# One decoder layer on one core: latents split from PSUM by two engines, row normalisation as one activation

## The reference, cut to what matters

```python
def _layernorm(x, axis=-1, eps=1e-05):
    m = jnp.mean(x, axis=axis, keepdims=True)
    v = jnp.var(x, axis=axis, keepdims=True)
    return (x - m) / jnp.sqrt(v + eps)

x = x + attn(_layernorm(x), wq, wk, wv, wo)          # causal, 32 query heads, 8 key heads, head size 16
x = x + xattn(_layernorm(x), ctx, Wq_d, W_qk, Wkv_d, Wv_u)
x = x + ffn(_layernorm(x), gate, kernel, bias, lora_A, lora_B, lora_A_shared, lora_B_shared)

def xattn(Q, K, Wq_d, W_qk, Wkv_d, Wv_u):
    C_kv = K @ Wkv_d                                 # the latents: 1500 x 32 for each sequence
    CqWqk = ((Q @ Wq_d) @ W_qk).reshape(b, n, 16, 32)
    scores = einsum('bnhl,bkl->bhnk', CqWqk, C_kv) / sqrt(32)
    V_up = (C_kv @ Wv_u).reshape(b, nkv, 16, 32)
    return einsum('bhnk,bkhd->bnhd', softmax(scores), V_up)
```

## Time and profile before

| | |
|---|---|
| median of three executions | 643.73 us (642.36 to 645.56) |
| the profiled execution | 645.84 us, span 644.0 us |
| mean granted TensorE clock | 0.968 |
| TensorE busy | 584.1 us, 91% |
| VectorE busy | 432.5 us, 67% |
| GpSimd busy | 412.7 us, 64% |
| ScalarE busy | 302.1 us, 47% |

### The profile page before, as it was taken

One profiled execution on the slowest core, in us unless ns is written; L12 is line 12 of the kernel. 1 busy time (PEld: TensorE's weight loads), 2 busy tenths in 40 slices (PEclk: granted clock), 3 DMA queues, 4 the chain that ended last, 5 costly groups with the idle time before them and its releaser, 6 DMA issues.

```text
span 644.0 us, 11508 instructions
## 1 busy us (share of the span) xinstructions
PE 584.1 (91%) x4164; PEld 315.5 (49%) x4164; DVE 432.5 (67%) x715; ACT 302.1 (47%) x642; POOL 412.7 (64%) x385
## 2 busy tenths in 40 slices
PE   7889797998999899999999899998999899988887
PEld 7436353455446354545446355455446355434445
DVE  2737964678757967778747957678757967656632
ACT  1421434537444555437444555437444555464460
POOL 5002166598758887598758887588758887789000
PEclk9997788899999999999999999999999999999899
DMA  9959511651048110751039110761039110200000
GB/s 320 409 107 348 208 36 24 251 206 35 12 120 317 59 45 22 268 204 39 9 108 336 52 45 22 253 219 32 16 93 334 68 45 23 64 19 0 24 2 15
DMA packets 31578, 77.40 MB, mean 120 GB/s; under 512 B 11297, under 2 KB 24961, under 8 KB 29218
## 3 DMA queue, kind: packets, MB, share of 16 engines
q1 hardware_dynamic: 30854, 75.27, 34.9%
q10 hardware_dynamic: 668, 1.40, 0.6%
HBM read 58.92 MB, written 2.88 MB: 96 GB/s over the span
## 4 chain that ended last, share of the span: by engine, by line
PE 58%; DVE 19%; ACT 6%; POOL 4%; SPq 4%; issue 4%; DMA 4%; ACTq 0%; POOLq 0%; DVEq 0%
PE st_ps L711 11%; PE mx_ps L754 9%; PE pv_ps L726 8%; PE mi_ps L496 4%; PE mi_ps L490 4%; DVE mx_p L1143 4%; POOL acc L1214 3%; PE mi_ps L503 3%; DVE p L1066 2%; PE mi_ps L586 2%; SPq L402 2%; DMA ctx_sb<-in_ctx_t 2%; DVE xn L1018 2%; PE mi_ps L590 2%; DVE p L1107 2%
## 5 line engine op out<-in xcount | busy, mean ns | idle before, releaser
L1214 POOL TENSOR_TENSOR acc<-acc,p_ring 125x448 f32<-125x448 f32 x290 | 348.0, 1200 | 65.4 <-ACT p_ring L941 25.8
L1143 DVE TENSOR_REDUCE mx_p<-mx_ps 128x1 f32<-128x500 f32 x336 | 210.0, 669 | 98.9 <-PE mx_ps L754 97.9
L941 ACT ACTIVATE p_ring<-st_ps 125x448 f32<-125x448 f32 x372 | 183.4, 544 | 151.6 <-PE st_ps L711 139.7
L711 PE MATMUL st_ps<-q_st,c_st 98*125 98x448 f32 x372 | 146.3, 432 | 9.8 <-ACT p_ring L941 8.6
L754 PE MATMUL mx_ps<-c_st,q_st 96*128 96x500 f32 x336 | 142.1, 457 | 12.2 <-DVE mx_p L1143 5.1
L711 PEld LDWEIGHTS st_ps<-q_st,c_st 98*125 98x125 f32 x372 | 65.3, 190 | 99.3 <-ACT p_ring L941 79.9
L726 PE MATMUL pv_ps<-p_ring,c_nat 125*32 125x448 f32 x768 | 94.5, 564 | 1.9 <-ACT ox L840 1.0
L754 PEld LDWEIGHTS mx_ps<-c_st,q_st 96*128 96x128 f32 x336 | 63.6, 197 | 43.7 <-DVE mx_p L1143 17.6
L1222 POOL TENSOR_TENSOR rstd<-mv,eps_col 128x1 f32<-128x1 f32 x24 | 4.6, 190 | 117.1 <-DVE mv L1014 116.6
L503 PE MATMUL mi_ps<-ctx_sb,wkv_sb 128*32 128x375 f32 x480 | 46.8, 511 | 5.5 <-DVE p L1066 5.5
L1214 POOL TENSOR_TENSOR acc<-p_ring 125x448 f32<-125x448 f32 x29 | 35.6, 1226 | 19.2 <-ACT p_ring L941 19.2
(11 more groups left out here) (137 smaller groups left out, 677.9 us busy)
## 6 DMA issues: line engine op xcount, KB each, us to landing
ctx_sb<-in_ctx_t SPq DMA_DIRECT2D x16, 3000.0 KB, 11.6
c_st<-ct_hl SPq DMA_DIRECT2D x192, 46.9 KB, 2.3
q_st<-q_hl SPq DMA_DIRECT2D x90, 56.0 KB, 2.0
x_sb<-in_x SPq DMA_DIRECT2D x8, 256.0 KB, 2.8
out_y<-x3n SPq DMA_DIRECT2D x16, 112.0 KB
wq_sb<-in_wq SPq DMA_DIRECT2D x2, 512.0 KB, 6.4
kern_sb<-in_lora_a SPq DMA_DIRECT2D x1, 1024.0 KB, 14.2
wo_sb<-in_wo SPq DMA_DIRECT2D x1, 1024.0 KB, 17.6
```

The lines of the kernel that those rows point to most:

```text
L711: mm(st_bank(unit)[0:KC, 0:HALF], c_st[:, b % 4, t * KT + k * KC:t * KT + (k + 1) * KC], q_st[:, b // 2 % 2, b % 2, half * HALF:(half + 1) ...
L941: act.activation(p_ring[:, unit % PR, :], st_bank(unit)[0:KC, 0:HALF], ACT.Exp, scale=float(L) ** -0.5).then_inc(exp_done, 1)
L1143: ve.tensor_reduce(mx_p[:, p:p + 1], mx_ps[unit % MXB][:, 0:KP], AX.X, ALU.max).then_inc(red_done, 1)
L1214: po.tensor_tensor(dst, first, p_ring[:, unit % PR, :].rearrange("p (h s) -> p h s", s=S), ALU.add).then_inc(acc_done, 1)
```

## The change

ScalarE's step A makes two copies out of PSUM, `ct_f` and the rounded high part `ct_hl[0]`. VectorE's step AS is one subtraction that reads the latents in PSUM and the high part. Since the transposes of CT write into the same bank, CT now waits for that subtraction (`a_lo`; not for sequence 0). In group 4 AS stands right behind A, and so ahead of SN0 on VectorE.

The normalisation becomes `activation(Identity, bias, scale)` on ScalarE, with rstd as scale and -mean x rstd as bias, both one value for each row. For this VectorE adds one instruction to the statistics (the negated mean), and GpSimd a third one to `power` (the product, `ln_shift`). N0 stays at the end of group 0; N1 runs after the third exponential (t = 2) of group 9 and N2 after the second (t = 1) of group 10. N0 and N1 of pair 0 stay on VectorE. The waits that VectorE gets for the previous normalisation (`ln[...]` in L0, W1 and YT) are for one that lies an iteration back.

```diff
@@ STEPS
-    [("SE0", "n"), ("Ah", "b"), ("MT", "m"), ("A", "b"), ("SE1", "n"), ("V", "n"), ("SN0", "n")],
-    [("CT", "b"), ("SN1", "n"), ("AS", "b")],
+    [("SE0", "n"), ("Ah", "b"), ("MT", "m"), ("A", "b"), ("AS", "b"), ("SE1", "n"), ("V", "n"),
+     ("SN0", "n")],
+    [("CT", "b"), ("SN1", "n")],
...
-    [("DN", "f"), ("Wh", "n"), ("M", 1), ("W1", "n"), ("M", 1), ("DT", "f"), ("N1", "n")],
-    [("YT", "f"), ("M", 1), ("T2", "n"), ("M", 1), ("CQ", "n"), ("M", 1), ("H", "n"), ("N2", "f")],
+    [("DN", "f"), ("Wh", "n"), ("M", 1), ("W1", "n"), ("M", 1), ("DT", "f")],
+    [("YT", "f"), ("M", 1), ("T2", "n"), ("M", 1), ("CQ", "n"), ("M", 1), ("H", "n")],
...
+N1_AT = 9
+def normal_at(i, g, t):
+    for (gn, tn), name, n in (((N1_AT, 2), "N1", i + 1), ((10, 1), "N2", i - 1)):
+        if (g, t) == (gn, tn) and 0 <= n < PAIRS:
+            yield name, n
@@ TensorE
                 elif name == "CT":
                     pe.wait_ge(a_f, n + 1)
+                    if n:
+                        pe.wait_ge(a_lo, n + 1)
@@ ScalarE
+            def normalise(which, n, src, dst):
+                act.wait_ge(ln_shift[which], n + 1)
+                act.activation(dst, src, ACT.Identity, bias=rstd[:, which, 2:3], scale=rstd[:, which, 1:2])\
+                    .then_inc(ln[which], 1)
...
                 elif name == "A":
+                    copy(ct_f[:, :], o[:, 0:KT]).then_inc(a_f, 1)
                     if n:
-                        act.wait_ge(a_lo, n)
-                    copy(ct_f[:, :], o[:, 0:KT]).then_inc(a_f, 1)
+                        act.wait_ge(cst_in[(n - 1) % 4], 16 * 12 * ((n - 1) // 4 + 1))
+                    copy(ct_hl[:, 0, :], o[:, 0:KT]).then_inc(a_hi, 1)
...
+                    for t in range(4):
+                        if 0 <= bs < B:
+                            exponential(bs, gg, t)
+                        for name, n in normal_at(i, g, t):
+                            step(name, n)
@@ VectorE
-                ve.bn_aggr(mv[:, which, :], stats[:, which, 0:6]).then_inc(s, 1)
+                ve.bn_aggr(mv[:, which, 0:2], stats[:, which, 0:6]).then_inc(s, 1)
+                ve.wait_ge(s, k + 2)
+                ve.tensor_scalar(mv[:, which, 2:3], mv[:, which, 0:1], -1.0, None, ALU.mult).then_inc(ln_neg[which], 1)
...
                 elif name == "AS":
-                    if n:
-                        ve.wait_ge(cst_in[(n - 1) % 4], 16 * 12 * ((n - 1) // 4 + 1))
-                    ve.wait_ge(a_f, n + 1)
-                    ve.tensor_copy(ct_hl[:, 0, :], ct_f[:, :]).then_inc(a_hi, 1)
                     ve.wait_ge(a_hi, n + 1)
-                    ve.tensor_tensor(ct_hl[:, 1, :], ct_f[:, :], ct_hl[:, 0, :].bitcast(F32), ALU.subtract)\
+                    ve.tensor_tensor(ct_hl[:, 1, :], step_bank("A", n)[:, 0:KT], ct_hl[:, 0, :].bitcast(F32),
+                                     ALU.subtract)\
                         .then_inc(a_lo, 1)
@@ GpSimd, power()
+                po.wait_ge(ln_pow[which], n + 1)
+                po.wait_ge(ln_neg[which], n + 1)
+                po.tensor_tensor(rstd[:, which, 2:3], mv[:, which, 2:3], rstd[:, which, 1:2], ALU.mult)\
+                    .then_inc(ln_shift[which], 1)
```

More of the change, by code:

```diff
@@ L221, in decoder_layer @@
         stats = sb("stats", [128, 3, 7])
-        mv = sb("mv", [128, 3, 2])
-        rstd = sb("rstd", [128, 3, 2])
+        mv = sb("mv", [128, 3, 3])
+        rstd = sb("rstd", [128, 3, 3])
         ident = sb("ident", [128, 128])
@@ L280, in decoder_layer @@
         ln_pow = [sem(f"ln_pow{n}") for n in range(3)]
+        ln_neg = [sem(f"ln_neg{n}") for n in range(3)]
+        ln_shift = [sem(f"ln_shift{n}") for n in range(3)]
         st_done = sem("st_done")
@@ L796, in _ @@
             step("W1", 0)
+            pe.wait_ge(a_lo, 1)
             lora_factors(3, 7)
@@ L840, in copy @@
                 return act.activation(dst, src, ACT.Copy, scale=scale)
+            def normalise(which, n, src, dst):
+                act.wait_ge(ln_shift[which], n + 1)
+                act.activation(dst, src, ACT.Identity, bias=rstd[:, which, 2:3], scale=rstd[:, which, 1:2])\
+                    .then_inc(ln[which], 1)
             def step(name, n, i=0, g=0):
+                if name == "N0":
+                    normalise(0, n, x_sb[:, n % 2, :], xn[:, :])
+                elif name == "N1":
+                    normalise(1, n, x2_sb[:, n % 2, :], xn[:, :])
+                elif name == "N2":
+                    normalise(2, n, x3[:, :], x3n[:, :])
                 if name == "XC":
@@ L922, in step, with exponential @@
                     copy(ax_t[0:2 * RANK, :], o[0:2 * RANK, 0:128]).then_inc(f1_sb, 1)
-            def exponentials(b, g):
-                half = g // KG
-                if b == 0 and g == 0:
+            def exponential(b, g, t):
+                unit = b * 24 + g * 4 + t
+                if unit == 0:
                     act.wait_ge(eff_out, 32)
[L929 to L942, removed]
+                act.wait_ge(st_done, unit + 1)
+                old = unit - PR
+                if old >= 0:
+                    act.wait_ge(pv_done, old // 4 + 1)
+                    added = (old // 24, old // 12 % 2)
+                    if added in DVE_HALVES:
+                        act.wait_ge(acc_dve, dve_adds(*added) + max(old % 12, 1))
+                    elif added != PE_HALF:
+                        act.wait_ge(acc_done, pool_adds(*added) + max(old % 12, 1))
+                act.activation(p_ring[:, unit % PR, :], st_bank(unit)[0:KC, 0:HALF], ACT.Exp,
+                               scale=float(L) ** -0.5).then_inc(exp_done, 1)
             def out_of_sums(b, half):
@@ L1028, in step @@
                     ve.wait_ge(x_in[slot], 16 * (n // 2 + 1))
+                    if n:
+                        ve.wait_ge(ln[0], 3 * n)
                     statistics(0, n, x_sb[:, slot, :])
[L1030 removed]
+                elif name == "N0" and n == 0:
                     normalise(0, n, x_sb[:, slot, :], xn[:, :])
[L1032 removed]
+                elif name == "N1" and n == 0:
                     normalise(1, n, x2_sb[:, slot, :], xn[:, :])
[L1034 to L1035 removed]
                 elif name == "AS":
[L1038 to L1041 removed]
                     ve.wait_ge(a_hi, n + 1)
[L1043 removed]
+                    ve.tensor_tensor(ct_hl[:, 1, :], step_bank("A", n)[:, 0:KT], ct_hl[:, 0, :].bitcast(F32),
+                                     ALU.subtract)\
                         .then_inc(a_lo, 1)
@@ L1069, in step @@
                 elif name == "W1":
+                    if n:
+                        ve.wait_ge(ln[1], 4 * n)
                     if n >= 2:
@@ L1085, in step @@
                 elif name == "YT":
+                    if n:
+                        ve.wait_ge(ln[2], 5 * n)
                     ve.wait_ge(y_out, 32 * n + 16)
```

4 lines of the change are left out of this document (1 added, 3 removed).

## The result

| | before | after |
|---|---|---|
| median of 11 executions each | 644.93 us (641.64 to 646.70) | 648.32 us (646.12 to 652.17) |
| ratio of the runs | 1 | 1.0064, interval 1.0043 to 1.0085 |
| profiled execution | 645.84 us, span 644.0 | 647.7 us, span 645.9 |
| mean granted TensorE clock | 0.968 | 0.970 |

The changed kernel is slower by 4.1 us (2.8 to 5.5): 0.64% of 645. The three executions shown beforehand are the first three of the eleven. The forecast was +5.5 us. One execution is left out of a ratio: 1798.73 us, one of the twelve of E7.

A forecast was written before the change was run, and what follows sets the result against it. TensorE was taken to bound the kernel, busy 67.84 of 71.93 us per iteration. Terms 6.7 - 2.4 + 0.5 + 0.7 = +5.5 us on the 643.73 us median gave 649.2 us, range 643 to 656.

The forecast's parts named there:

- N0: End of group 0: group 1's exponentials queue behind it on ScalarE, CT 1.12 us later in six iterations, +6.7 us.
- N1: Group 9: it ends sooner on ScalarE, so T2 starts 0.34 us earlier, seven times, -2.4 us.
- N2: Group 10: free in ScalarE's idle time; last pair +0.5 us; pair 6 set to 0 within 1 us.
- nothing gives it back: Group 1: TensorE has no idle time until the self attention's scores, so CT's 1.12 us delay stays.
- The activation: Normalisation on ScalarE: 0.63 us copy plus 0.13 for two operands, 0.76 us; other estimate 0.82; bounds 0.63 and 1.35.
- delays nothing: Negated mean on VectorE, 0.15 to 0.35 us, runs beside the 0.89 us until rstd is ready: no cost.
- Latents: Groups 4 and 5: VectorE's shed cast and subtraction gain 0; CT of sequence 1 waits in first iteration, +0.7 us.
- Absorbed: Rival: group 1's lost time returns in TensorE's idle time in groups 4 and 5; -1.2 us, 642.5 us; chance 0.12.
- GpSimd set free: Rival: relieved VectorE lets GpSimd's additions run sooner, 10.6 us of exponentials' waits go; 638.6 us; chance 0.07.
- Slow activation: Rival: the normalisation on ScalarE takes 1.35 us; sum +13.9 us, 657.6 us; chance 0.05.
- Table loads: Rival: Identity in another table than Exp, 22 normalisations each loading twice; +56 us, about 700 us; chance 0.02.
- Clock: Rival: group 1's idle time drops TensorE's clock to 1.2 GHz in six iterations, up to 1.75 us each; 659.7 us; chance 0.10.

The follow-up runs named there:

- E7: Kernel before with only N2 moved to ScalarE, for all pairs but the first iteration's: 647.74 us, ratio 1.0059 to the kernel before.
- E1: Kernel after with N0 back on VectorE, without its negated mean and shift: 642.48 us, ratio 0.9965 to the kernel before.
- E2: Kernel after with N0 on ScalarE run later, behind the second exponential of group 1: 642.73 us, ratio 0.9952 to the kernel before.
- E8: Kernel after with N0 a plain copy of x behind the same wait, nothing normalised there: 647.64 us in one execution; copy 0.63 us.
- E6: Kernel before with only N1 of pairs 1 to 7 moved to ScalarE: 644.96 us, ratio 1.0000 to the kernel before.
- E3: Kernel before with the latents' part of the change alone, all normalisations on VectorE: 638.3 us, ratio 0.9884 to the kernel before.
- E5: Kernel before with only N0 of pairs 1 to 7 moved to ScalarE, end of group 0: 657.25 us, ratio 1.0192 to the kernel before.
- E11: Kernel after with GpSimd's shift of N0 computed three times over, so N0 comes later: 658.35 us, ratio 1.0218 to the kernel before.
- E9: Kernel before with the latents' part, and the latents' negated maxima moved behind VectorE's second score half in group 3: 639.27 us, ratio 0.9924.

## Why the prediction came out right, and where it was wrong

- **N0: the queue right, its last link not quite.** 1.12 us at CT were forecast, 1.18 measured, by the queue that was described. E1 and E2 show it by its removal and by its place. The last link was "nothing gives it back". A little is given back: where `x` came late, and 0.31 us in each iteration between SB and CT "b" (E1), so that 0.86 stay.
- **The activation: 0.81 us, forecast 0.76.** VectorE's price for operands (132 ns) was too low for ScalarE; E8 gives 0.18 us. The Trainium skill (ScalarE: Activation LUTs, What ACT_TABLE_LOAD costs) had 93 ns for each, which this agrees with. The prediction's other estimate, 0.82 us, was the nearer one, but its sentence on the sum is wrong: 0.06 us more raise the loss in six places and lower the gain in seven, and both add to the time, so the sum rises by some 0.8 us to 6.3, and not by under 0.2.
- **N1: the mechanism right, the gain not kept.** T2 after YT gained 0.49 for the forecast's 0.34. The step that failed is that the negated mean "delays nothing": it delays VectorE's reciprocal in group 8, and TensorE's transposes of `y_t` with it, by 0.2 us in each of six iterations. The rest is lost at YT's addition, which I had not followed: it moved forward onto a GpSimd addition. E6: 0 for the forecast -2.4. In the kernel after N2's negated mean does it once more: T2 to T3 is 6.49 there and 6.28 in E6. The maxima stand behind it on VectorE, and TensorE waits for them by 0.22 us longer, as the rows below this list show (the kernel after, then E6, where N2 is on VectorE).
- **N2: the middle right, the last one right (0.53 for 0.5), pair 6 wrong.** I set the queued exponentials off against VectorE's freedom, "0 within 1 us". It was +1.6, and because of that freedom (E7).
- **Latents: wrong in sign.** CT of sequence 1 was held as forecast (51.22, forecast 51.4), and T1 moved by 0.4 and not 0.7. The step that failed is "VectorE sheds the cast ... and the subtraction, and TensorE was not waiting for either: 0". I had read that in a middle iteration. In the first one TensorE stood for 2.01 us behind them, and in every one `xn` was behind the cast of "a". E3: -7.5 for +0.7.
- **The sum.** By runs: latents -7.5, N1 and N2 on top +5.2 (E1 less E3, 0.81%), N0 on top of these +6.4; together +4.1. By the intervals each of these is known to some 2 us; E6 and E7 give 0 and +3.8 for N1 and N2 one by one, but N0 alone gives +12.4 (E5), so the parts don't simply add up. The forecast +5.5 was near by luck: two misses of opposite sign, 8 us too much for the latents and 7 too little for N1 and N2, nearly cancel. The range held for the same reason.
- **Rivals.** Absorbed: refuted in the main by E1, as 0.86 of N0's 1.18 us stay, but its mechanism exists, in group 4, for 0.31. GpSimd set free: refuted by the waits, 12.2 us for 10.6; in E3, with the lowest median, they are even 16.9 us. Slow activation: 0.81 us, not 1.35. Table loads: the kernel after still loads once. Clock: not in this kernel at 0.88 us of idle time, but E5 and E11 show it. The price of 1.75 us was read too high: of the longer iteration in the earlier trace rows the fall of the clock made 1.07 and a late `x` the other 0.69. A fall in E5 cost 1.3 to 1.6.

The maxima behind the mean of N2, TensorE's weight load with its wait:

```profile
246.82 0.15 DVE L1045 TENSOR_SCALAR mv<-mv 128x1 f32<-128x1 f32 x1
246.89 1.84 DVE L1175 TENSOR_REDUCE mx_p<-mx_ps 128x1 f32<-128x500 f32 x3
...
247.61 0.19 PEld L769 LDWEIGHTS mx_ps<-c_st,q_st 96*128 96x128 f32 x1 [0.39 <-DVE mx_p L1175]
```
```profile
248.32 0.19 PEld L767 LDWEIGHTS mx_ps<-c_st,q_st 96*128 96x128 f32 x1 [0.17 <-DVE mx_p L1178]
```

What stays open: how much of the first iteration's gain is the latents' and how much the clock's, whose falls lie at other places in each kernel. E9 shows that the 0.57 us in group 4 moves, not what would end it.

## What to carry to other kernels

Moving an instruction to an idle engine costs what is queued behind it there: put it where its input is already waiting, and count the time for its extra operands (here the shift, a negated mean and two hand-overs) before its start. An engine that is relieved runs ahead and meets another engine's work at new places, so follow the first instructions behind each gain. Look for a wait in the first and last iterations too before an edit is set to nothing.
